# Layer 1's attention start: five value products moved behind the first maxima, the maxima's transfer ahead of loads, bias products and statistics moved

## The reference

```
q = layernorm(x) @ Wq + bq
k, v = split(context @ Wkv + bkv)
scores = einsum('bhid,bhjd->bhij', q, k) * 16 ** -0.5
out = softmax(scores) @ v
x = x + out @ Wout + bout
```

## Time and profile before

| what | value |
|---|---|
| runs (median of three) | 1242.67 us (1241.54, 1242.67, 1252.23) |
| profiled execution | 1248.94 us, its span 1247.2 us |
| TensorE busy | 1107.5 us (89% of the span) |
| VectorE busy | 751.6 us (60%) |
| ScalarE, GpSimd busy | 527.8 us (42%), 474.8 us (38%) |
| mean granted TensorE clock | 0.929 of full speed |
| layer 1's attention, from the first value product to the last values | 599.4 to 895 us |

### The profile page before, as it was taken

One profiled execution on the slowest core, in us unless ns is written; L12 is line 12 of the kernel. 1 busy time (PEld: TensorE's weight loads), 2 busy tenths in 40 slices (PEclk: granted clock), 3 DMA queues, 4 the chain that ended last, 5 costly groups with the idle time before them and its releaser, 6 DMA issues. The chain is left out here.

```text
span 1247.2 us, 20458 instructions
## 1 busy us (share of the span) xinstructions
PE 1107.5 (89%) x6708; PEld 761.6 (61%) x6709; DVE 751.6 (60%) x1466; ACT 527.8 (42%) x1074; POOL 474.8 (38%) x518
## 2 busy tenths in 40 slices
PE   4788877699999999999658899998878999999997
PEld 1244444599999999999523444454545455555554
DVE  6878668367458557643467887876067244444427
ACT  4266653345336335522326666666324122323210
POOL 4203430556356546421335354102014066656510
PEclk9599987799999999999859999989568999999999
DMA  5122213533133123120343132320381422222242
GB/s 176 28 93 93 78 46 98 194 127 111 52 117 127 61 83 128 53 96 18 102 111 116 57 104 87 103 87 2 127 303 53 167 72 72 77 80 77 56 168 102
DMA packets 68048, 121.63 MB, mean 98 GB/s; under 512 B 16993, under 2 KB 36232, under 8 KB 67206
## 3 DMA queue, kind: packets, MB, share of 16 engines
q1 hardware_dynamic: 57894, 96.28, 23.6%
q0 software_dynamic: 10080, 24.38, 6.1%
HBM read 89.84 MB, written 33.82 MB: 99 GB/s over the span
## 5 line engine op out<-in xcount | busy, mean ns | idle before, releaser
L739 ACT ACTIVATE PT<-S 128x512 f32<-128x512 f32 x384 | 203.8, 599 | 124.3 <-PE S L717 123.3
L754 DVE TENSOR_REDUCE M<-S 128x2 f32<-128x1024 f32 x192 | 225.2, 1219 | 34.4 <-PE S L693 33.9
L510 PE MATMUL bankm<-XSTh,w12h 128*128 128x320 f32 x512 | 163.2, 319 | 5.3 <-DVE HF L594 5.2
L510 PE MATMUL bankm<-XSTl,w12h 128*128 128x320 f32 x512 | 159.7, 312 | 0.0
L510 PE MATMUL bankm<-XSTh,w12l 128*128 128x320 f32 x512 | 159.6, 312 | 0.0
L693 PE MATMUL S<-KS,QS 62*128 62x512 f32 x384 | 92.6, 498 | 43.2 <-DVE M L754 18.0
L588 DVE TENSOR_TENSOR HTl<-HF,HTh 128x320 fp32r<-128x320 f32 x128 | 129.7, 1013 | 1.0
L2199 PE MATMUL bank<-W,XST 128*128 x248 | 121.0, 610 | 4.6 <-issue 1.3
L717 PE MATMUL S<-QS,KS 64*128 64x512 f32 x384 | 112.0, 491 | 5.9 <-DMA QS<-NM 5.2
L727 PE MATMUL PV<-PT,VA 128*32 128x256 f32 x1536 | 109.6, 406 | 3.7 <-ACT PT L739 2.4
L554 ACT ACTIVATE SG<-bankm 128x320 f32<-128x320 f32 x128 | 56.1, 438 | 117.0 <-PE bankm L510 115.9
(11 more groups left out here) (274 smaller groups left out, 2008.6 us busy)
## 6 DMA issues: line engine op xcount, KB each, us to landing
stage<-in_W12T SPq DMA_DIRECT2D x32, 512.0 KB
stage<-in_W3T SPq DMA_DIRECT2D x16, 512.0 KB
W<-in_fc1T SPq DMA_DIRECT2D x2, 3840.0 KB, 18.8
YG<-yk SPq DMA_DIRECT2D x4, 1536.0 KB, 12.4
yk<-zeros SPq DMA_DIRECT2D x4, 1024.0 KB, 4.7
KS<-scrk SPq DMA_DIRECT2D x32, 128.0 KB, 2.7
scrq<-parts SPq DMA_DIRECT2D x16, 256.0 KB
QS<-scrq SPq DMA_DIRECT2D x30, 128.0 KB, 2.5
```

Of the source, the lines that this page charges most:

```text
L510: m = pe.matmul(bank[:, c % 2, 0:HALF], ew.w12[a][s][:, k, f:f + P], XST[b][:, k, half * HALF:(half + 1) * HALF], start=(k == 0 and (a, b) ...
L739: act.activation(self.PT[:, kt, 2 * j + h, :], self.S2[:, n % 3, :], ACT.Exp, scale=self.lay.scale).then_inc(self.exp_done, 1)
L754: dve.tensor_reduce(self.M[:, g % 2, :, h, q], got, AX.X, ALU.max).then_inc(self.ring.dve_free, 1)
```

## The change

- TensorE: 11 of the 16 value products stay in front (EARLY), the other five stand one each behind maxima units 1 to 5 of group 0. The bias products go from ahead of the first unit of group 1 to behind the turn of the maxima. The turn of XN(1) goes from block (0, 0) to (0, 2).
- ScalarE: slots 0 and 1 of KS are filled behind the eighth copy of values; the last five copies stand behind high(0,1), with slot 2's fill behind the first of them and slot 3's behind the last.
- VectorE: its half of the pick goes ahead of low(0,1); statistics and seed of batch 1 go behind the negation. In layer 0, the statistics of batch 3 likewise.
- GpSimd: the memset of QS's slots 1 and 2 no longer waits; that of slot 3 waits for all value products.
- SP queue: K of groups 0 and 1 together, then both stores, then Q of group 1, K and Q of group 2, and the shift. The waits for the last fill and the last memset stand ahead of the loop.

The first of the two new memsets follows that of VA directly; the wait stands between the two. The diff:

```diff
@@ module level
-FRONT0, FRONT1 = AHEAD, UNITS + 2
+FRONT0, FRONT1, EARLY = AHEAD, UNITS + 2, 11
-TURN_XN, QUERY = {(0, 0): 1, (0, 15): 2, (1, 15): 3}, {(0, 3): (1, 0), (0, 4): (1, 1), (1, 0): (2, 0), (1, 8): (2, 1),
+TURN_XN, QUERY = {(0, 2): 1, (0, 15): 2, (1, 15): 3}, {(0, 3): (1, 0), (0, 4): (1, 1), (1, 0): (2, 0), (1, 8): (2, 1),
@@ layer0, vector
             low_keys(1)
-            first_stats(3)
             keep_values(1)
...
             at.negate(dve, 0)
+            first_stats(3)
@@ layer1, sync
             at.load(sp, 0, "k")
+            at.load(sp, 1, "k")
+            store(0, 0)
+            store(0, 1)
+            sp.wait_ge(zeros_done, 1)
+            load(1, "q")
             sp.wait_ge(ones_done, 2)
-            at.load(sp, 1, "k")
-            sp.wait_ge(zeros_done, 1)
-            store(0, 0)
-            load(1, "q")
-            store(0, 1)
             at.load(sp, 2, "k")
             load(2, "q")
             at.shift(sp, 0)
...
+            sp.wait_ge(zeros_done, 2)
+            sp.wait_ge(ones_done, 3)
@@ layer1, gpsimd
+            pool.memset(at.QS[:, 1:SLOTS - 1, :, :].bitcast(F32), 0.0).then_inc(zeros_done, 1)
             pool.wait_ge(v_ready, NT)
-            pool.memset(at.QS[:, 1:, :, :].bitcast(F32), 0.0).then_inc(zeros_done, 1)
+            pool.memset(at.QS[:, SLOTS - 1, :, :].bitcast(F32), 0.0).then_inc(zeros_done, 1)
@@ layer1, tensor
-            for t in range(NT):
+            for t in range(EARLY):
                 value(t)
...
-            pe.wait_ge(v_done, NT)
+            pe.wait_ge(v_done, EARLY)
...
             for u in range(UNITS):
                 at.maxima(pe, 0, u)
+                if 1 <= u <= NT - EARLY:
+                    value(EARLY + u - 1)
+            at.maxima(pe, 1, 0)
+            at.turn(pe, 0)
             pe.wait_ge(wo_loaded, 32)
             pe.wait_ge(bvb_done, KD)
...
-            at.maxima(pe, 1, 0)
-            at.turn(pe, 0)
@@ layer1, scalar
-            for t in range(NT):
+            for t in range(EARLY):
                 keep_value(t)
-            fill_keys(slice(0, 1), 1)
+                if t == 2 * TPB - 1:
+                    fill_keys(slice(0, 2), 2)
...
-            fill_keys(slice(1, SLOTS), SLOTS - 1)
+            for t in range(EARLY, NT):
+                keep_value(t)
+                if t == 3 * TPB - 1:
+                    fill_keys(slice(2, 3), 1)
+            fill_keys(slice(3, 4), 1)
@@ layer1, vector
             low(0, 0)
-            low(0, 1)
             dve.wait_ge(at.picked, 2)
             dve.tensor_copy(at.QS[:, 0, 1, :], at.S2[:, 1, :]).then_inc(at.dve_stack, 1)
-            dve.wait_ge(added, 2 * PER)
-            link(norm_tiles(dve, pre, X, range(TPB, 2 * TPB)))
-            norm_seed(dve, link, pre, 1)
+            low(0, 1)
...
             at.negate(dve, 0)
+            dve.wait_ge(added, 2 * PER)
+            link(norm_tiles(dve, pre, X, range(TPB, 2 * TPB)))
+            norm_seed(dve, link, pre, 1)
```

## The result

The changed kernel took 1236.91 us (median of 20 executions, 1228.42 to 1250.81), the kernel before, measured beside it, 1248.64 us (20 executions, 1239.84 to 1254.34). The ratio is 0.9909 with an interval of 0.9884 to 0.9933: 0.9% faster, less than the 1% that the forecast lay just beyond. The three longest of the changed kernel's 20 executions (1246.99 to 1250.81 us) count as slow and are left out of the ratio. The forecast's own ratio is 1229.0 / 1242.67 = 0.9890, inside the interval. The three runs shown before the forecast lay low among the 20, so ratios are compared here, not the two absolute times. The profiled execution took 1234.19 us with a span of 1232.5, against 1248.94 and 1247.2: 14.7 less, where the sum had 13.7.

What follows compares the result with a forecast made beforehand. TensorE bounds the long stages, but a chain over all engines bounds layer 1's attention start. Gains of 11.4, 0.9 and 1.4 sum to 13.7 us, off the median 1242.67 giving 1229.0; range 1222 to 1239.

Steps and rivals of the forecast that it cites:

- the sum: Whole kernel: layer 1's scores 11.4, turn of XN(1) 0.9 and layer 0 1.4, together 13.7 us gained.
- some 0.6 of the 4.2 is lost: Layer 1's turn of XN: five moved values free 4.2 us, but the new memset delays VectorE and XN, losing 0.6.
- Queries, pick, first reduction: Start of layer 1's attention: queries 3.8 us earlier, first maxima 1.4 more from the pick, first reduction 6.6 earlier.
- the first rival: Layer 1's queries and picks run at the lower clock, costing some 3.5 us; gain 10.2, time 1232.5; chance 0.2.
- So the values are hidden there, and I add 0.1: Layer 1's eight reductions: value products fit between maxima pairs at the upper clock, adding 0.1 us to 9.14.
- NM and the transfer: Layer 1: negated maxima 8.6 us earlier, SP queue free for their transfer, first scores 11.4 earlier.
- the rival that the transfer isn't ahead in effect: SP queue: Q of group 1 lands late or loads still precede the transfer; gain about 11.2, time 1231.5; chance 0.1.
- I take 0.9: Turn of XN(1), moved two blocks later in layer 1's scores: between nothing and 1.9 us gained, taken as 0.9.
- Layer 0: Layer 0's statistics behind the negation: cast's wait and idle time saved, less about 0.4; 1.4 us gained, bounds 0 and 2.6.
- The clock did fall before the scores: Rival for layer 1's first blocks: no clock fall before the scores, up to 4 us more gained, 1225.0; chance 0.12.
- The thinned blocks: Rival: without the turn, layer 1's first score blocks stay at the lower clock, 2.1 us more each; chance 0.05.
- The values at the lower clock: Rival: value products among layer 1's maxima run at the lower clock, 5 us lost, gain 8.7, 1234.0; chance 0.13.

Runs made afterwards that it cites:

- stats_turn_old: Changed kernel with batch 1's statistics back ahead of the reductions and the turn of XN(1) back in the first block; 1235.72 us, ratio 0.9915.
- bias_late: Changed kernel with GpSimd adding the bias to batch 0 of X only in the second group; 1227.13 us (0.9856), second time 1231.03 us (0.9875).
- values_front: Changed kernel with all 16 value products in front again, fills as changed; 1243.18 us, ratio 0.9961 to the kernel before.
- sp_old: Changed kernel with the SP queue's old order of loads and stores; 1243.63 us, ratio 0.9969 to the kernel before.
- bo_front: Changed kernel with the bias products back ahead of group 1's first maxima and the turn; 1237.87 us, ratio 0.9918.
- l0_only: Kernel before with layer 0's edit alone (statistics of batch 3 behind the negation); 1248.01 us, ratio 1.0017.
- memset_late: Changed kernel with GpSimd waiting for XN of batch 0 before the memset of QS's slots 1 and 2; 1234.40 us, ratio 0.9891.
- both: Changed kernel with the late memset of QS and the late bias addition on GpSimd together; 1229.17 us, ratio 0.9906.
- both_ten: Changed kernel with late memset, late bias addition and ten value products in front instead of eleven; 1229.19 us, ratio 0.9857.
- no_l0: Changed kernel with layer 0's edit undone, the rest kept; 1236.01 us, ratio 0.9920 to the kernel before.

## Why the prediction was right, and where its terms were off

**The turn of XN: right in size, wrong in its reason.** It starts 11.82 behind the values (forecast 11.7). The block by the new memset came as forecast: L122 and L123 took 0.95 and 1.73, and the second ended 0.02 behind the memset. But it cost nothing in this execution, since the values in front took 11.98. Before, the eleventh ended 11.1 in; the clock rose 3.0 behind the start there, and 4.6 behind it after, so more of them ran at 1.2 GHz. That the two came to the same time is luck. The step "some 0.6 of the 4.2 is lost" named VectorE's chain, and the late memset, which cleared that chain, left the turn at the values' end. Only with an early rise, in `stats_turn_old`, did XN bind, by 0.36.

**Queries, pick, first reduction: right.** 3.8 forecast and 3.82 measured at the queries (14.02 behind the values against 17.84). The second `bias_late`, with the clock up after 3.2 and so nearly as early as before, has 13.43, 4.4 gained; so the late rise hid a part of the gain. At the first maxima it was 5.2 forecast and 5.3 measured, at the first reduction 6.6 and 6.74. No queries at the lower clock: the first rival fell. There was no idle time ahead of the turn, and 1.16 behind it.

**"So the values are hidden there, and I add 0.1": the term that was mis-sized.** The eight reductions took 10.53 (30.92 - 20.39), not 9.24. A unit is 1.49, from 618.84 to 620.33 to 621.82: 0.43 from the pair's start to the value's, and 1.06 from the value's to the next pair's. I had taken 0.86 for a value from a row of values only, and 0.2 to 0.4 for a pair. Why the two take longer in turn isn't shown. So TensorE, not VectorE, bounds these five units: 5 x (1.49 - 1.14) = 1.75, less what the first units lie ahead. `values_front`, without them, has 9.18. The move still pays, 2.65 at the scores, or some 3.2 at like clock, where the forecast had 4.2 - 0.6 - 0.1 = 3.5.

**NM and the transfer: right.** NM came 7.6 earlier for 8.6 forecast, all of the difference being the mis-sized units. The transfer is issued at once, and the scores start 2.85 behind the issue (2.88 before). The old order in `sp_old` costs 8.4: the rival that the transfer isn't ahead in effect fell. Behind the turn the bias products are hidden, and `bo_front` shows 2.3 for the old place. So 10.5 of the forecast 11.4 at the scores.

**"I take 0.9" for the turn of XN(1): wrong in sign.** From the first scores to the third turn it is 31.7 after, and 29.6 before: 2.1 lost. Its parts are visible. Up to the second turn it is 10.82 against 11.19, from there 20.88 against 18.43.

The first two blocks are 1.2 shorter without the turn of XN(1), but 0.83 of that is lost again. The addition of the bias on GpSimd stands at 640.07 to 642.84 behind XN(1), which itself comes later because the statistics do, and VectorE's second cast now falls into it; moved away in `bias_late`, 0.83 of the second turn came back. The Trainium skill, "SBUF — State Buffer", section "Who interferes with whom", says that a cast of VectorE can need the port pair that it shares with GpSimd, and that whoever issues second waits until the other's instruction is through. By that rule, the trace agrees: the two ends are 0.03 apart.

The rest is in the one block where the turn now stands: at 648.29 it takes 1.50, in a stretch with the clock at 0.50 from 645.8, and VectorE then waits 2.81 for the next pair. From the start of this block's scores to the next it is 6.37, where the block without a turn took 3.81. `sp_old` separates the place from the clock. It has the turn and the statistics in their new places, no wait of the cast, and the clock up in this block: 10.00 to the second turn and 19.73 on to the third, together 29.73 against 29.62 before. So with the clock up the block grows by 1.3 for a turn of 1.09, because TensorE's idle time in it, 1.16 as in the kernel before, stands ahead of the last maxima and the turn behind them, where nothing hides it; and the 1.2 gained in the first two blocks pays for it: the new place is worth nothing, where the forecast had 0.9. The cast's wait, 0.83, and the lower clock in the block, 20.88 - 19.73 = 1.15, make up the 2.1. `stats_turn_old` agrees: with the old places the third turn comes 29.97 behind the scores. But that kernel pays 6.2 ahead of them.

**Layer 0: 1.4 forecast, about 2 in the trace, nothing in the time.** The scores of layer 0 start 3.0 earlier, of which 0.8 was there already at the first query products (14.20 against 14.97), before the change acts. The 2.2 that the stretch from the first maxima gives are the two terms of the forecast, less its 0.4, and what it hadn't counted: ahead of the reductions VectorE idled 0.21, and a tensor_scalar (L124) took 0.43 instead of 0.17, both gone now. At layer 1's start the difference is 2.55, less than what two executions with the same layer 0 can differ by. A new block of the same kind came with it: the second cast took 2.12, ending with the zeros' memset, but VectorE idled behind it anyway. `l0_only` shows 1.0017, so whatever it gains is below what ten executions tell.

**The sum.** 10.5 at layer 1's scores, less 2.1 to the third turn, and 2.55 from layer 0, make 11.0, which is what the matched third turn shows, and what stays, 10.8, up to the negated maxima at 807.8 (797.0 after). The remaining 3.9 of the profile's 14.7 come later, where the clock of the two executions differs: 2.7 of them at the next two, at 823.7 and 836.8, around a fall of the clock in the kernel before from 820.8 to 827.6. The medians show 11.7, with the interval's ends at 8.4 and 14.5. So the 13.7 lies within what was measured, and its parts made up for each other: at the third turn layer 1 has 10.5 - 2.1 = 8.4 where the forecast had 11.4 + 0.9 = 12.3, and layer 0 has 2.55 where it had 1.4. Whether the change is beyond 1%, as the forecast's time had it, the interval leaves open: 0.9% by its middle.

**The other rivals.** The clock did fall before the scores (at 628.7), so they didn't start at 2.4 GHz. The thinned blocks didn't come in this execution: the clock rose at 642.3, ahead of the turn that was said to be needed for it, and the fall from 645.8 to 649.2 was short. But the rival isn't refuted. In seven of the eleven traces with the turn in its new place (`values_front`, `bo_front`, `memset_late`, `both`, `both_ten` and both of `bias_late`) the clock stayed at 0.50 until 16.0 to 19.5 behind the scores, that is until the turn of XN(1), at 15.9 to 16.6, had begun; in the three with the turn in its old place it rose after 6.1 to 12.3. The third turn comes 31.3 to 33.2 behind the scores there, and 29.6 to 30.3 here; that the move of the turn causes it isn't shown. The values at the lower clock didn't occur here, but in `stats_turn_old`, and in part in `sp_old`.

## What to carry to other kernels

Work put between the steps of a chain is priced by the unit that then results on each engine, with the alternation in it, and not by the duration it has among its own kind: 0.86 became 1.06 here, and the pair beside it 0.43. When an engine's work is moved, look at what its neighbours run at the new time, even at instructions of 0.17 us, and whether they have slack: of the two blockers here, moving the addition on GpSimd brought 0.83 at the next turn, and moving the memset nothing where the values were the later. In a block where an engine's work stands in line, a moved piece costs its full length again, even if another engine seems to bound the block. And measure an edit of 2 us at the instruction it moves, in the trace, with the granted clock beside it, before asking the whole time about it.

## What the runs showed of the hardware

The whole time goes with the mean granted clock. Over the 20 executions of the changed kernel the two have a correlation of -0.95, with 7.2 us for each 0.01 of clock: 1228.42 us at 0.945, 1250.81 at 0.918. Two executions of the changed kernel show a place where it is decided, at the end of layer 1's attention and behind it. The two traces stay within 0.3 us of each other from the first negated maxima of layer 1 to 851; then the clock falls in both at 860.8 and rises at 877.8 in the first and at 874.4 in the second. What follows is, in the first:

```profile
884.00:885.00 1.00, 1.00 (x7) 0.90 (x5) 0.00 (x0) 0.00 (x0) 0.00 (x0) 0.50 1.10 352
```

and in the changed kernel taken again:

```profile
884.00:885.00 1.00, 1.00 (x6) 0.88 (x5) 0.00 (x0) 0.00 (x0) 0.00 (x0) 1.00 1.10 351
```

At the comparison `eq` they are 5.5 apart (924.77 and 919.23), and their spans differ by 5.1. In the first, the clock was at 0.50 from 863 to 877 with TensorE busy for 13.74 of 14 us (last window above); in the kernel with both edits it was up in a window of the same length near there, with TensorE less busy:

```profile
866.00:880.00 14.00, 10.57 (x101) 5.65 (x100) 1.59 (x5) 7.91 (x16) 0.00 (x0) 1.00 0.33 108
```

So a full TensorE is no sign of the upper clock, and the same program meets both in the same stage. What decides between them isn't shown. This is part of why `stats_turn_old` can stand level with a kernel whose scores come 6.2 earlier: its ten executions had a mean clock of 0.941, and the changed kernel's 20 had 0.936. If each execution is shifted to a mean clock of 0.935 with the slope found within kernels (7.4 us for 0.01), the kernel before stands at 1244.7, the changed one at 1239.1, `stats_turn_old` at 1240.9, the late addition of the bias at 1235.9 and 1236.8, both edits at 1235.8 and both with ten in front at 1237.3. The changed kernel's gain is then 5.6. By the same measure `values_front` (1238.8) and `no_l0` (1238.9) are level with it, `memset_late` has 1238.2, `bo_front` 1240.6, and `l0_only` (1243.4) and `sp_old` (1243.5) are little ahead of the kernel before; a mean is uncertain by 0.3 to 0.9. So the 8.4 of the queue shows in the whole time, as 4.4, and the 2.65 of the moved values doesn't.

This measure takes off too much, however, because the mean clock isn't independent of the change: around the first scores, the kernel before stands at 0.50 for 30.7 us (626.3 to 657.0) and the changed one for 17.0 (13.6 and 3.4). The 13.7 us less raise its mean clock by half of 13.7 in 1240, 0.0055, and the shift takes back 4.1 us for that. By this estimate from the two profiles, 5.6 + 4.1 = 9.7 is the change's own, near the 10.8 of the matched instructions. Whether the some 2 that remain of the 11.7 come through a later clock that the earlier scores bring about isn't shown. Nor is it shown why adding the bias late gives 2 to 3 in this measure, when the traces have only 0.8 of it in the first groups.
